# A four-layer graph network on one core: TensorE signals from a drain instead of from the last matmul

## The chip, the cores and the metric

The kernel runs on 1 core of one Trainium2 chip. The metric is the device time of one execution in microseconds; before the change the median of 3 runs is 5,466.43 us.

## What is computed

A graph of 6,250 nodes with 128 features and 200,000 edges goes through four pre-norm residual layers. `dst` is sorted, `src` is random.

```python
h = max(layernorm(x), 0); x = x + L0(h)   # h @ Wa.T + mean of h[src] over dst @ Wb.T + b
h = max(layernorm(x), 0); x = x + L1(h)   # sum over edges of w*(h[dst]-h[src]), w = sigmoid(relu((h[dst]-h[src])@W1+b1)@W2+b2); + indeg*(h@W4+b4)
h = max(layernorm(x), 0); x = x + L2(h)   # mean of relu(h@Wp.T+bp)[src] @ Wl.T + bl + h@Wr.T, elu, normalised, + h
h = max(layernorm(x), 0); x = x + L3(h)   # sum over edges of (h @ weight[etype])[src]*norm; + h@loop_weight
```

## The kernel before

The edges lie in 1,563 tiles of 128, one edge a partition, and tiles go in groups of four (`TPG`). There are two ways to sum over a destination.

The first is **gather and scatter**. POOL issues one indirect DMA per tile (line 1470) that fetches the 128 source rows from a table in HBM. VectorE builds a one-hot matrix of the destinations of each tile within a window of 128 nodes (lines 1863, 1869). TensorE multiplies the one-hot matrix with the gathered rows and accumulates in PSUM (`scatter`, lines 2530, 2533, 2537; `scatter_h`, 2511). The last matmul of a group increments `s_scat`. POOL waits for `s_scat` before it gathers into the group's slot again (5 slots in layers 0 and 2, 7 in layer 1, 10 in layer 3), VectorE before it writes a one-hot buffer again. When a window is full, it is copied, turned with the identity (`far_turn`, 2546 and 2548, `s_gturn`) and added to `acc`.

The second is **counting**. Where destinations are dense, VectorE writes pairs of one-hot matrices (1954, 1955, 1960, 1961), TensorE turns them into counts of edges between a block of sources and a few destinations (`count`, 2559, `s_count`), ScalarE takes the counts out (1632), and a pack matmul multiplies them with the node table (`pack_mm`, 2574, then 2584 and 2586). Layer 0 makes the early counts and multiplies at once. Layer 1 makes the late counts for layer 2 and stores them, layer 2 loads all of them.

Layer 1 has a longer chain for each group: SyncE fetches the destinations (`dst_flat`), VectorE makes a turned one-hot (1990), TensorE expands the destination rows (`expand`, 2597, `s_expand`), VectorE subtracts and weights (1998, 2003, "hidden"), ScalarE sums and takes the sigmoid (1681, 1686, "gates"), VectorE makes the gated one-hot (1863), TensorE scatters. Expansion stands one turn behind the gather, hidden and gates two, the scatter four.

Layer 3 has **dense steps** beside its gathers: `count3` (2469, 148 times), `mult3` (2481), `rels3` (2490), `put3` (2499), the latter three once for each of 13 bundles. VectorE's `pair3` (1908, 1909) waits for the count3 three tiles back. Between layers 2 and 3 lies a short stage of gathers for the heads (116 tiles), beside the relation products (2419).

All engines walk one list `plan`, written out by Python generators, and each engine's program takes its own kinds of step from it in that order. A planner's credit spreads the pack work evenly over the turns of groups. Every signal is a semaphore increment; on TensorE it is attached to the last matmul of a step:

```python
for t in range(m):
    last = pe.matmul(far3_banks[v % 3][:, 0:P], rows[:, slot, t, :], oneh[:, g % NONE_F, t, :],
                     start=start, stop=stop)
last.then_inc(s_scat.handle, 1)
```

Of the kernel before, what the change touches and what calls it, by code (L numbers as in the profile page):

```python
# [11 lines left out]
P = 128  # L12
TPG = 4
WIN = 64
# [51 lines left out]
def gnn_program(nc, ins, out):  # L66
# [15 lines left out]
    while len(bundles) < npk and (not bundles or bundles[-1][-1] < npk - 1):  # L82
        k0 = bundles[-1][-1] + 1 if bundles else 0
        n = max(m for m in range(1, npk - k0 + 1) if m * needed[k0 + m - 1] <= BUNDLE)
# [15 lines left out]
    while not heads or heads[-1][-1] < HEAD_END - 1:  # L100
        a = heads[-1][-1] + 1 if heads else ng3
        n = max([m for m in range(1, HEAD_END - a + 1) if n_nodes * (2 * a + m) * m * TPG * TPG <= HEAD_SPAN * nt * nt] + [1])
# [44 lines left out]
    with ExitStack() as ctx:  # L147
# [2202 lines left out]
        def tensor_program(pe):  # L2350
            pe.wait_ge(s_const.handle, n_const)
            for kind, st in plan:
# [110 lines left out]
                elif kind == "count3":  # L2463
# [4 lines left out]
                    for b, (q0, q1) in enumerate(((0, st["half"]), (st["half"], nb))):  # L2468
                        last = pe.matmul(ps[st["bank"] + b][:, 0:(q1 - q0) * w3], srow3[:, slot, :],  # L2469
                                         pairs3[:, slot, q0 * w3:q1 * w3], start=st["start"], stop=st["stop"])  # L2470
                    last.then_inc(s_count3.handle, 1)
                elif kind == "mult3":
                    q0, q1, width = st["q0"], st["q1"], st["width"]
                    if q0 == 0:
# [5 lines left out]
                    for q in range(q0, q1):  # L2480
                        last = pe.matmul(ps[4][:, 0:width], h[:, q, :], weights3[:, q, 0:width], start=q == 0, stop=q == nb - 1)  # L2481
                    if q1 == nb:
                        last.then_inc(s_mult3.handle, 1)
                elif kind == "rels3":
                    pe.wait_ge(s_sum3.handle, st["sum"])
                    if st["out_free"]:
# [2 lines left out]
                    for r in range(n_rel):  # L2489
                        last = pe.matmul(ps[4][0:st["slots"], P:2 * P], by_rel[:, :, r], wrel[:, r * P:(r + 1) * P],  # L2490
                                         start=r == 0, stop=r == n_rel - 1)
                    last.then_inc(s_rels3.handle, 1)
                elif kind == "put3":
                    n = st["slots"]
                    pe.wait_ge(s_place3.handle, st["place"])
                    pe.wait_ge(s_out3.handle, st["out"])
                    if st["add_free"]:
                        pe.wait_ge(s_add.handle, st["add_free"])
                    pe.matmul(ps[4][:, 2 * P:2 * P + WIN], out3[0:n, :], place[0:n, st["u"] % 2, 0:WIN], start=True, stop=True
                              ).then_inc(s_put3.handle, 1)  # L2500
                elif kind == "scatter_h":
                    g, m, slot = st["g"], tiles[st["g"]], st["slot"]
                    pe.wait_ge(s_one.handle, st["one"])
# [6 lines left out]
                    for t in range(m):  # L2510
                        last = pe.matmul(far3_banks[st["bank"]][:, 0:P], rows[:, slot, t, :], oneh[:, g % NONE_F, t, :],
                                         start=st["first"] and t == 0, stop=st["last"] and t == m - 1)
                    last.then_inc(s_scat.handle, 1)
                elif kind == "rels_h":
                    pe.wait_ge(s_hsum.handle, st["copy"])
                    by_rel = sums_head[:, st["half"], 0:st["n"] * P].rearrange("p (c r) -> p c r", r=n_rel)
                    for r in range(n_rel):
                        last = pe.matmul(far3_banks[st["bank"]][:, P:P + st["n"] * HEAD_WIN], wrel[:, r * P:(r + 1) * P], by_rel[:, :, r],
                                         start=r == 0, stop=r == n_rel - 1)
                    last.then_inc(s_hrel.handle, 1)  # L2520
                elif kind == "scatter":
                    g, v, m, slot = st["g"], st["v"], tiles[st["g"]], st["slot"]
                    pe.wait_ge(s_one.handle, st["one"])
                    pe.wait_ge(s_row[slot].handle, st["row"])
                    if st["first"] and st["add"]:
                        pe.wait_ge(s_add.handle, st["add"])
                    for t in range(m):
                        start, stop = st["first"] and t == 0, st["last"] and t == m - 1
                        if st["layer"] == 3:
                            last = pe.matmul(far3_banks[v % 3][:, 0:P], rows[:, slot, t, :], oneh[:, g % NONE_F, t, :],  # L2530
                                             start=start, stop=stop)
                        elif st["layer"] == 1:
                            last = pe.matmul(far_banks[v % 2][:, 0:P + 1], oneh[:, g % NONE_F, t, :],  # L2533
                                             rows_hp[slot][:, t, P:2 * P + 1], start=start, stop=stop)
                        else:
                            n_part = 3 * P + 1 if st["sums"] == 2 else 3 * P
                            last = pe.matmul(far_banks[v % 2][:, 0:n_part], onehb[:, g % NONE, t, :], rows_h3[slot][:, t, 0:n_part],  # L2537
                                             start=start, stop=stop)
                    last.then_inc(s_scat.handle, 1)
                elif kind == "far_turn":  # L2540
                    bank = far_banks[st["v"] % 2]
                    if st["layer"] == 1:
                        pe.wait_ge(s_glo.handle, st["lo"])
                    else:
                        pe.wait_ge(s_gev.handle, st["hi"])
                    last = pe.matmul(bank[:, 0:P], gsum[:, 0:P], ident[:, :], start=True, stop=True)
                    if st["sums"] == 2:
                        last = pe.matmul(bank[:, P:2 * P], gsum[:, P:P + 1].to_broadcast([P, P]), ident[:, :],
                                         start=True, stop=True)
                    last.then_inc(s_gturn.handle, 1)  # L2550
                elif kind == "count":
                    i, w, start, stop = st["i"], st["w"], st["start"], st["stop"]
                    pe.wait_ge(s_pair.handle, st["pair"])
                    for bank, q0, q1, evicted, signals, _ in st["parts"]:
                        if evicted:
                            pe.wait_ge(s_cev.handle, evicted)
                        rows_of_source = srow_late if st["late"] else srow
                        pair = pairs_late[:, i % 2, :] if st["late"] else pairs[:, i % NQS, :]
                        last = pe.matmul(ps[2 + bank][:, 0:(q1 - q0) * w], rows_of_source[:, i % NSR, :], pair[:, q0 * w:q1 * w],  # L2559
                                         start=start, stop=stop)  # L2560
                        if signals:
                            last.then_inc(s_count.handle, 1)
                elif kind == "pack_mm":
                    u, width, q0, q1 = st["u"], st["width"], st["q0"], st["q1"]
                    n_part = 3 * P + 1 if st["sums"] == 2 else 3 * P
                    if q0 == 0:
                        if st["layer"] == 0:
                            pe.wait_ge(s_cev.handle, st["cev"])
                        else:
                            pe.wait_ge(s_cld[u % 2].handle, st["cld"])  # L2570
                        if st["wev"]:
                            pe.wait_ge(s_wev.handle, st["wev"])
                    for q in range(q0, q1):
                        last = pe.matmul(ps[st["bank"]][0:width, 0:n_part], counts[:, u % 2, q, 0:width], h3[:, q, 0:n_part],  # L2574
                                         start=q == 0, stop=q == nb - 1)
                    if q1 == nb:
                        last.then_inc(s_pack.handle, 1)
                elif kind == "pack_turn":
                    u, width = st["u"], st["width"]
                    pe.wait_ge(s_place.handle, st["place"])  # L2580
                    pe.wait_ge(s_wev.handle, st["whi"])
                    if st["added"]:
                        pe.wait_ge(s_add.handle, st["added"])
                    last = pe.matmul(ps[1][:, 0:P], wsum[0:width, 0:P], place[0:width, u % 2, :], start=True, stop=True)
                    if st["sums"] == 2:
                        last = pe.matmul(ps[1][:, P:2 * P], wsum[0:width, P:P + 1].to_broadcast([width, P]),
                                         place[0:width, u % 2, :], start=True, stop=True)
                    last.then_inc(s_turn.handle, 1)
                elif kind == "expand":
                    g = st["g"]  # L2590
                    m, sl = tiles[g], g % 2
                    pe.wait_ge(s_oneT.handle, st["oneT"])
                    pe.wait_ge(s_pw[st["v"] % 2].handle, st["pw"])
                    if st["hid"]:
                        pe.wait_ge(s_hid.handle, st["hid"])
                    for t in range(m):
                        last = pe.matmul(ps_t[sl][:, t * P:(t + 1) * P], onehT[:, sl, t * P:(t + 1) * P], pwin[:, st["v"] % 2, :],  # L2597
                                         start=True, stop=True)
                    last.then_inc(s_expand.handle, 1)
                elif kind == "general":  # L2600
                    flag = outside_flag(pe, st["layer"])
                    with pe.If(flag):
                        general_tensor(pe, st["layer"], st["sums"])
                    if st["layer"] == 1:
                        pe.wait_ge(s_onecol.handle, 1)
# [29 lines left out]
```

## Time and profile before

| | |
|---|---|
| median of 3 runs | 5,466.43 us (5,464.44 to 5,467.47) |
| profiled execution, span | 6,426.8 us (its page gives no other time of it) |
| busy: PE, PEld, DVE, ACT, POOL | 60%, 46%, 46%, 22%, 62% of the span |
| mean granted TensorE clock | 0.761 |
| stages by POOL's gathers | layer 0: 107.8 to 1,217.8; layer 1: 1,304.2 to 3,643.1; layer 2: 3,696.3 to 4,293.8; heads: 4,340.8 to 4,510.9; layer 3: 4,526.4 to 6,404.8 us |

PE is TensorE's matmuls, PEld its weight loads, DVE VectorE, ACT ScalarE, POOL GpSimd, SP SyncE. The span of the profiled execution is 960 us longer than the median run. Busy time of PE is the union of matmuls whose ends are modelled. A tile's name in the rows is that of the memory under it (`third`, `rows`, `oneh`, `turned_words` are reused by several stages). "remote", or "another core or an unknown queue", is a wait whose releaser the trace does not tell. An f32 matmul of the program stands in the trace as two MATMUL rows with two LDWEIGHTS.

### The profile page before, as it was taken

The page shows a single profiled execution, that of the slowest core. Times are in us where ns is not written, and L with a number is a line of the kernel's source. Part 1 is how long each engine was busy: PE and PEld are TensorE (multiplying, and loading weights), DVE is VectorE, ACT ScalarE, POOL GpSimd, SP SyncE. Part 2 cuts the span into 40 slices and gives each one's busy share as a digit, 9 for nine tenths or more (in the row PEclk, how much of TensorE's full clock was granted, in tenths as well). Part 3 has the DMA queues.
Part 4 walks back from the last instruction along what each step waited for, and adds up shares of the span by engine and source line. Part 5 has one row for each costly group of instructions (what it writes and reads, how often), then busy time and mean ns, then how long its engine had stood idle before and what let it go on. Part 6 is the DMA issues. An engine that isn't in the chain of part 4 may idle for free.

```text
span 6426.8 us, 68888 instructions
## 1 busy us (share of the span) xinstructions
PE 3872.2 (60%) x20122; PEld 2959.4 (46%) x20154; DVE 2933.5 (46%) x9989; ACT 1413.8 (22%) x5474; POOL 3972.3 (62%) x4198
## 2 busy tenths in 40 slices
PE   4676766655555565555555578876565565665433
PEld 3333434445544454455455456653344444444332
DVE  7555544556555565556555633342333222222222
ACT  4222122333333333333333401121000000000000
POOL 4556666456666666666666466646566666666665
PEclk7778778777777777777777789998777777777666
DMA  3333333345455454544545455555211111111121
GB/s 107 96 101 110 111 105 116 107 140 155 143 150 148 147 150 144 154 145 141 159 144 151 123 184 198 195 181 178 69 46 46 45 47 45 46 45 46 46 61 46
DMA packets 323521, 734.49 MB, mean 114 GB/s; under 512 B 77056, under 2 KB 164124, under 8 KB 310860
## 3 DMA queue, kind: packets, MB, share of 16 engines
q0 software_dynamic: 172432, 405.32, 23.2%
q1 hardware_dynamic: 148700, 323.81, 14.9%
q8 instruction: 168, 2.75, 0.2%
q14 instruction: 205, 1.68, 0.1%
q10 hardware_dynamic: 2016, 0.92, 0.1%
HBM read 598.71 MB, written 131.05 MB: 114 GB/s over the span
## 4 chain that ended last, share of the span: by engine, by line
another core or an unknown queue 30%; PE 27%; DVE 19%; issue 15%; ACT 4%; DMA 2%; DVEq 1%; SPq 1%; ACTq 0%
PE ps L2574 8%; DVE oneh L1863 6%; PE ps L2559 3%; PE ps L2530 3%; PE ps L2537 2%; DVE ps L1998 2%; PE ps L2469 2%; PE ps L2597 2%; DMA third<-dst_flat 2%; ACT turned_words L1681 1%; DVE third L1990 1%; PE ps L2419 1%; DVE turned_words L1955 1%; DVE tmp L1954 1%
## 5 line engine op out<-in xcount | busy, mean ns | idle before, releaser
L1470 POOL DMA_INDIRECT rows<-tab_rel,third x1299 | 1247.0, 960 | 646.9 <-issue 367.1
L1470 POOL DMA_INDIRECT rows<-tab_h,idx_src x1086 | 1046.7, 964 | 723.4 <-issue 345.8
L1470 POOL DMA_INDIRECT rows<-tab_hp,idx_src x1120 | 1077.1, 962 | 622.5 <-issue 298.8
L2597 PE MATMUL ps<-third 128*128 128x128 f32 x3126 | 607.1, 353 | 501.6 <-issue 295.8
L2530 PE MATMUL ps<-oneh,rows 128*128 128x128 f32 x2598 | 489.1, 340 | 607.1 <-DVE oneh L1863 330.7
L2597 PEld LDWEIGHTS ps<-third 128*128 128x128 f32 x3126 | 539.6, 258 | 593.7 <-issue 355.3
L2574 PE MATMUL ps<-third,h 128*120 128x384 bf16 (+17 forms) x3773 | 715.0, 337 | 65.8 <-issue 34.6
L2530 PEld LDWEIGHTS ps<-oneh,rows 128*128 128x128 f32 x2598 | 432.6, 245 | 695.8 <-DVE oneh L1863 362.6
L1681 ACT ACTIVATE turned_words<-turned_words 128x128 f32<-128x128 f32 x1563 | 463.1, 300 | 690.8 <-DVE turned_words L2003 527.5
L2574 PEld LDWEIGHTS ps<-third,h 128*120 128x120 bf16 (+10 forms) x3773 | 487.8, 133 | 239.4 <-issue 61.3
L1470 POOL DMA_INDIRECT third<-tab_hp,idx_src x443 | 425.9, 961 | 231.7 <-issue 118.5
L1863 DVE TENSOR_SCALAR oneh<-iota_b,dst_rel,third 128x128 f32<-128x128 f32 x1299 | 356.5, 356 | 306.5 <-remote 244.6
L2533 PE MATMUL ps<-rows,oneh 128*128 128x129 f32 x2240 | 413.5, 333 | 90.6 <-issue 86.7
L1863 DVE TENSOR_SCALAR oneh<-iota_b,dst_rel,gate 128x128 f32<-128x128 f32 x1563 | 445.1, 359 | 17.0 <-ACT gate L1686 15.2
L2533 PEld LDWEIGHTS ps<-rows,oneh 128*128 128x128 f32 x2240 | 376.7, 248 | 102.1 <-issue 100.0
L2559 PE MATMUL ps<-turned_words,tmp 128*128 128x504 bf16 (+10 forms) x1108 | 330.0, 366 | 143.2 <-issue 69.5
L1632 ACT CAST h<-ps 128x245 bf16<-128x245 f32 (+13 forms) x554 | 233.1, 448 | 828.5 <-PE ps L2559 468.0
L1954 DVE TENSOR_SCALAR tmp<-tmp 128x128 bf16<-128x128 int16 x872 | 230.5, 265 | 312.4 <-PE ps L2559 168.4
L1998 DVE TENSOR_TENSOR ps<-ps,rows 128x512 f32<-128x512 f32 x280 | 193.7, 692 | 389.0 <-remote 318.3
L2481 PE MATMUL ps<-acc,h 128*128 128x128 f32 (+1 forms) x1274 | 219.3, 320 | 127.4 <-issue 94.6
L1681 ACT ACTIVATION_READ_ACCUMULATOR turned_words<-turned_words 128x1 f32 x1563 | 296.0, 189 | 0.0
L1955 DVE TENSOR_SCALAR turned_words<-tmp,key 128x245 bf16<-128x245 int16 (+10 forms) x872 | 289.9, 333 | 0.0
(279 smaller groups left out, 5495.4 us busy)
## 6 DMA issues: line engine op xcount, KB each, us to landing
third<-dst_flat SPq DMA_DIRECT2D x390, 256.0 KB
h<-cnt_d SPq DMA_DIRECT2D x48, 1568.0 KB
cnt_d<-h SPq DMA_DIRECT2D x29, 1568.0 KB
cnt_d<-third SPq DMA_DIRECT2D x19, 1568.0 KB
tab_rel<-third SPq DMA_DIRECT2D x49, 512.0 KB
rows<-tab_rel,third POOLq DMA_INDIRECT x1299
rows<-tab_hp,idx_src POOLq DMA_INDIRECT x1120
rows<-tab_h,idx_src POOLq DMA_INDIRECT x1086
```

Of the source, the lines that this page charges most:

```text
L1470: pool.indirect_dma_start(out=to[:, t, 0:n], out_offset=None, in_=table[:, :], in_offset=bass.IndirectOffsetOnAxis(ap=idx[:, col:col + 1], ...
L1632: act.copy(to[:, q0:q1, place:place + w], ps[2 + bank][:, 0:(q1 - q0) * w].rearrange("p (q w) -> p q w", w=w)).then_inc(s_cev.handle, 1)
L1681: last = act.activation(v, v, ACT.Copy, accum_out=zed[:, sl, t:t + 1])
L1863: last = dve.tensor_scalar(oneh[:, g % NONE_F, t, :], iota_b[:, :], dst_rel[:, col:col + 1], by, ALU.is_equal, ALU.mult)
L1954: dve.tensor_scalar(srow[:, i % NSR, :], iota_k[:, 0:P], src_row[:, i:i + 1], None, ALU.is_equal)
L1955: dve.tensor_scalar(pairs[:, i % NQS, 0:nb * w], iota_k[:, 0:nb * w], key[:, i:i + 1], None, ALU.is_equal).then_inc(s_pair.handle, 1)
L1998: dve.tensor_tensor(out=v, in0=v, in1=rows_hp[st["slot"]][:, 0:m, 0:P], op=ALU.subtract).then_inc(s_diff.handle, 1)
L2530: last = pe.matmul(far3_banks[v % 3][:, 0:P], rows[:, slot, t, :], oneh[:, g % NONE_F, t, :], start=start, stop=stop)
L2533: last = pe.matmul(far_banks[v % 2][:, 0:P + 1], oneh[:, g % NONE_F, t, :], rows_hp[slot][:, t, P:2 * P + 1], start=start, stop=stop)
L2559: last = pe.matmul(ps[2 + bank][:, 0:(q1 - q0) * w], rows_of_source[:, i % NSR, :], pair[:, q0 * w:q1 * w], start=start, stop=stop)
L2574: last = pe.matmul(ps[st["bank"]][0:width, 0:n_part], counts[:, u % 2, q, 0:width], h3[:, q, 0:n_part], start=q == 0, stop=q == nb - 1)
L2597: last = pe.matmul(ps_t[sl][:, t * P:(t + 1) * P], onehT[:, sl, t * P:(t + 1) * P], pwin[:, st["v"] % 2, :], start=True, stop=True)
```

## The change

Each place named below ends with a `drain` on TensorE that carries the increment, in place of the increment on the last matmul. A drain is an instruction of the queue that ends when the engine's earlier work is done, and what stands behind it in TensorE's queue starts after it. Early counts (layer 0), pack matmuls, their turn, and all node-wise steps keep their signals on the matmul. The order of instructions on every engine, and the number of matmuls, stay. In the built program there are 2,188 new drains: 988 behind `scatter`, 29 behind `scatter_h`, 391 behind `expand`, 444 behind late `count`, 145 behind `far_turn`, 148 behind `count3`, 13 each behind `mult3`, `rels3` and `put3`, 4 behind `rels_h`.

```diff
@@ count3, mult3, rels3, rels_h, scatter_h, scatter, far_turn, expand
-                    last.then_inc(s_count3.handle, 1)
+                    pe.drain().then_inc(s_count3.handle, 1)
...
-                        last.then_inc(s_mult3.handle, 1)
+                        pe.drain().then_inc(s_mult3.handle, 1)
...
-                    last.then_inc(s_rels3.handle, 1)
+                    pe.drain().then_inc(s_rels3.handle, 1)
...
-                    pe.matmul(ps[4][:, 2 * P:2 * P + WIN], out3[0:n, :], place[0:n, st["u"] % 2, 0:WIN], start=True, stop=True
-                              ).then_inc(s_put3.handle, 1)
+                    pe.matmul(ps[4][:, 2 * P:2 * P + WIN], out3[0:n, :], place[0:n, st["u"] % 2, 0:WIN], start=True, stop=True)
+                    pe.drain().then_inc(s_put3.handle, 1)
...
-                    last.then_inc(s_scat.handle, 1)
+                    pe.drain().then_inc(s_scat.handle, 1)
...
-                    last.then_inc(s_hrel.handle, 1)
+                    pe.drain().then_inc(s_hrel.handle, 1)
...
-                    last.then_inc(s_gturn.handle, 1)
+                    pe.drain().then_inc(s_gturn.handle, 1)
@@ count
-                        if signals:
+                        if signals and st["late"]:
+                            pe.drain().then_inc(s_count.handle, 1)
+                        elif signals:
                             last.then_inc(s_count.handle, 1)
@@ expand
-                    last.then_inc(s_expand.handle, 1)
+                    pe.drain().then_inc(s_expand.handle, 1)
```

## Rows read from the trace of the kernel before

**Rows 1.** The timeline of 4571 to 4600 us, POOL: start, length, instruction, idle before.
```profile
4576.14 0.94 POOL L1470 DMA_INDIRECT rows<-tab_rel,third  x1 [0.30 <-issue]
4577.39 0.94 POOL L1470 DMA_INDIRECT rows<-tab_rel,third  x1 [0.30 <-issue]
```

**Rows 2.** The line of the gathers, L1470: count, duration min/median/max in ns.
```profile
L1470 POOL DMA_INDIRECT rows<-tab_rel,third x1299: 938/944/1404, 4526.4 to 6403.8; - x186
L1470 POOL DMA_INDIRECT rows<-tab_hp,idx_src x1120: 940/946/1431, 1304.2 to 3638.4; - x187
L1470 POOL DMA_INDIRECT rows<-tab_h,idx_src x1086: 940/946/2048, 107.8 to 4292.9; - x181
L1470 POOL DMA_INDIRECT third<-tab_hp,idx_src x443: 940/946/1437, 1329.8 to 3642.2; - x148
```

**Rows 3.** The table of stages: busy us and count of each engine, granted clock.
```profile
core 0: us, PE busy (x) PEld busy (x) DVE busy (x) ACT busy (x) POOL busy (x), PEclk, DMA share, GB/s
0.00:107.80 107.80, 46.52 (x218) 38.66 (x219) 72.83 (x283) 53.74 (x117) 52.37 (x120) 0.81 0.47 137
107.80:1217.80 1110.00, 731.28 (x3481) 411.63 (x3481) 606.36 (x2681) 257.23 (x627) 667.90 (x691) 0.76 0.35 103
1217.80:1304.20 86.40, 63.32 (x386) 52.30 (x385) 53.56 (x260) 39.89 (x97) 11.82 (x15) 0.80 0.44 133
1304.20:3643.10 2338.90, 1339.03 (x7451) 1176.17 (x7481) 1340.63 (x3646) 800.24 (x3956) 1503.81 (x1564) 0.75 0.50 147
3643.10:3696.30 53.20, 20.11 (x123) 18.21 (x123) 39.03 (x104) 32.27 (x89) 0.02 (x1) 0.66 0.29 96
3696.30:4293.80 597.50, 498.86 (x2910) 367.31 (x2911) 220.83 (x1010) 66.72 (x203) 378.64 (x395) 0.93 0.57 193
4293.80:4340.80 47.00, 26.08 (x136) 17.90 (x134) 27.92 (x125) 25.52 (x73) 0.84 (x3) 0.75 0.44 141
4340.80:4510.90 170.10, 120.38 (x413) 63.32 (x412) 51.48 (x128) 33.41 (x64) 109.93 (x116) 0.83 0.53 180
4510.90:4526.40 15.50, 12.71 (x55) 8.69 (x54) 8.48 (x27) 2.87 (x6) 0.01 (x1) 0.89 0.45 175
4526.40:6404.80 1878.40, 1002.83 (x4895) 795.09 (x4893) 502.44 (x1691) 101.88 (x244) 1247.00 (x1299) 0.71 0.19 47
6404.80:6426.80 22.00, 11.05 (x67) 10.13 (x67) 9.98 (x37) 0.00 (x0) 0.00 (x0) 0.73 0.07 19
```

**Rows 4.** The same timeline, layer 3, PE and DVE around a late signal.
```profile
4574.55 1.48 PE L2469 MATMUL ps<-third 128*128 128x400 f32 x4
...
4591.12 0.28 DVE L1908 TENSOR_SCALAR third<-iota_b,turned_words 128x128 f32<-128x128 f32 x1 [17.62 <-remote]
```

**Rows 5.** The page: busy time by engine, and the chain's shares.
```profile
PE 3872.2 (60%) x20122; PEld 2959.4 (46%) x20154; DVE 2933.5 (46%) x9989; ACT 1413.8 (22%) x5474; POOL 3972.3 (62%) x4198
...
another core or an unknown queue 30%; PE 27%; DVE 19%; issue 15%; ACT 4%; DMA 2%; DVEq 1%; SPq 1%; ACTq 0%
```

**Rows 6.** POOL's waits, layer 1, then layer 3: us in total, times, longest.
```profile
POOL rows L1470 <- remote: 233.6, 115, 4.7
...
POOL third L1470 <- remote: 93.5, 48, 2.8
POOL rows L1470 <- PE ps L2533: 71.0, 26, 5.8
...
POOL rows L1470 <- remote: 228.8, 81, 5.9
POOL rows L1470 <- PE ps L2530: 27.0, 15, 4.2
```

**Rows 7.** The timeline in layer 1: ends of scatter groups and the next weight load.
```profile
2012.45 1.93 PE L2533 MATMUL ps<-rows,oneh 128*128 128x129 f32 x8
...
2013.96 0.36 PEld L2559 LDWEIGHTS ps<-tmp 128*128 128x128 bf16 x2
...
2016.52 1.12 PE L2533 MATMUL ps<-rows,oneh 128*128 128x129 f32 x8
...
2017.36 0.21 PEld L2559 LDWEIGHTS ps<-tmp 128*128 128x128 bf16 x2
```

**Rows 8.** The timeline in layer 2: end of a scatter group.
```profile
3906.72 0.81 PE L2537 MATMUL ps<-rows,oneh 128*128 128x384 bf16 x4
...
3907.21 1.02 PEld L2441 LDWEIGHTS ps<-wlT,acc 128*128 128x128 f32 x8
```

**Rows 9.** Lines L2524 and L147, PE's sequencer: duration ns min/median/max.
```profile
L2524 PEldq EVENT_SEMAPHORE  x784: 51/51/51, 142.0 to 6418.4; - x196
...
L147 PEldq DRAIN  x1: 687/687/687, 6421.4 to 6421.4; - x1
```

**Rows 10.** PE's groups by line in layer 2 (3696.3 to 4293.8 us).
```profile
L2574 PE MATMUL ps<-third,h 128*120 128x384 bf16 (+10 forms) x2270 | 418.6, 337 | 47.6 <-DMA h<-cnt_d 23.8 <-issue 23.2
...
L2546 PE MATMUL ps<-ident,gsum 128*128 128x128 f32 x56 | 11.3, 277 | 3.2 <-issue 3.2
```

More of the change, by code:

```diff
@@ L2538, in tensor_program @@
                                              start=start, stop=stop)
-                    last.then_inc(s_scat.handle, 1)
+                    pe.drain().then_inc(s_scat.handle, 1)
                 elif kind == "far_turn":
```

## The prediction

> **What bounds the kernel now.** I read the stage table first, then the gather line, POOL's waits, and a piece of the timeline where a signal is late. POOL issues one indirect gather per tile of 128 edges, and its rows show a fixed pace: a descriptor step of 0.94 us and 0.30 us of issue, so the starts stand 1.25 us apart [rows 1]. There are 4,064 gathers: 1,299 + 1,120 + 1,086 + 443 from tables [rows 2] and 116 in the heads stage [rows 3]. 4,064 x 1.25 = 5,080 us. The turnovers before, between and behind the five gather stages take 107.8 + 86.4 + 53.2 + 47.0 + 15.5 + 22.0 = 331.9 us [rows 3]. A kernel in which POOL never waits inside a stage would thus last 5,080 + 332 = 5,412 us.
>
> The profiled execution lasts 6,426.8 us, 1,015 us above that ledger, and the median run 5,466.4 us, only 54 us above it. The page gives no time of that execution beside its span. So nearly all that POOL waits in the profile is absent from the undisturbed runs, provided POOL's pace is the same there (a software loop with 0.94 us in every stage makes that likely; no row proves it). This is the reading on which everything below rests.
>
> What the extra 960 us are made of can be seen at one place. The last dense-step matmuls, count3, start at 4574.55 and end at 4576.03; then PE has nothing in flight, yet VectorE's L1908, which waits for a dense-step signal of PE, goes on only at 4591.12, after 17.62 us that the trace puts on a releaser it doesn't know [rows 4]. A signal of finished matmuls was at least 15 us late while PE stood idle. The same "unknown" makes 30% of the chain of waits [rows 5], and POOL's waits in layers 1 and 3 are mostly of that kind [rows 6]. The drain would look like the cure. But the ledger says that the undisturbed run can hold at most 54 us of such lateness inside the stages. I take it as mostly the profiler's own: PE has 40,276 of the 68,888 recorded instructions [rows 5]. The Trainium skill (NOTIFIC — the notification-queue block, section 7.1) has a rule of this kind: the block that writes the trace records holds its producers back inside rather than lose a record. It names no figure, and no row here shows the block itself.
>
> **The change, part by part.** It adds 2,188 drains to PE's queue, takes 2,188 increments off matmuls, and moves nothing. They are 1,017 behind scattered groups (a group is up to four tiles: 173, 391, 99, 29 and 325 in the stages' order), 391 behind expansions, 444 behind late counts, 145 behind far turns, 187 behind dense steps, 4 behind the heads' relation sums.
>
> *Price of one drain.* No row shows a drain inside a stream of PE, so I bound it. What it forbids is visible. In layer 1 at the slow clock a group of 8 matmuls starts at 2012.45 and takes 1.93, to 2014.38, while the next weight load has begun at 2013.96: 0.42 us of overlap [rows 7]. At the fast clock: 2016.52 + 1.12 = 2017.64 against 2017.36, 0.28 us. In layer 2, bf16: 3906.72 + 0.81 = 3907.53 against 3907.21, 0.32 us [rows 8]. The drain takes that overlap away. Its own step costs at least a sequencer's, 0.05 us [rows 9]; the drain at the program's end took 0.69 us, waiting included. Lower bound 0 (where PE would wait next anyway), upper bound 0.69 + 0.42 = 1.1 us; I take overlap plus 0.05: 0.33 us warm f32, 0.37 us in layer 2, 0.47 us cold. The Trainium skill (TensorE: Matmul & The Clock Gate, section "Part 2: What happens when you issue a matmul") puts the part of one matmul's latency that a following one hides at about 0.175 us; by that figure, an estimate, the layer 2 term below would be 127 x 0.175 = 22 us instead of 47.
>
> *Layer 2 (3696.3 to 4293.8).* POOL's 395 gathers need 395 x 1.25 = 494 us; PE is busy 498.9 us there, at a clock of 0.93 [rows 3]: PE is as full as POOL. It carries 2,270 of the pack matmuls for 418.6 us beside the scatters [rows 10]. 99 groups and 28 turns (56 matmuls of L2546 [rows 10], two a turn) add 127 drains x 0.37 = 47 us. There is no cover for them. PE's 499 + 47 = 546 us becomes the bound. I take three quarters, +35 us, since some drains fall where PE waits for a load (23.8 us before pack matmuls [rows 10]) or for VectorE.
>
> *Layer 0 (107.8 to 1217.8).* POOL needs 691 x 1.25 = 864 us, PE is busy 731.3 [rows 3]. 173 scatters and 44 turns: 217 x 0.37 = 80 us, to 811. Early counts keep their matmul signals. Cover 133 us; cost 0, with up to 20 us where several engines take turns.
>
> *Layer 1 (1304.2 to 3643.1).* 391 scatters, 391 expansions, 444 late counts and 65 turns: 1,291 drains, at 0.33 to 0.47 us 426 to 607 us of PE. PE is busy 1,339 of the profile's 2,339 us, and POOL needs 1,563 x 1.25 = 1,954 [rows 3]. PE would hold 1,765 to 1,946 us of that. The cover is 1,954 - 1,339 = 615 us, used to between 70% and nearly all. The group's chain runs expansion, VectorE's hidden step, ScalarE's gates, one-hot, scatter; its slots give POOL seven groups less the four that the scatter lies behind. Behind a drain wait the next expansion and its VectorE step. Cost 0 in the likeliest case, up to +80 if the slow clock holds.
>
> *Heads and layer 3.* Heads: 29 groups x 0.47 = 14 us on 120 of PE against POOL's 145 [rows 3]; hidden. Layer 3: 325 + 187 = 512 x 0.47 = 241 us on 1,002.8, together 1,244 against POOL's 1,299 x 1.25 = 1,624; hidden.
>
> *Late signals removed.* Worth between 0 and the 54 us above; I take 0 in the sum.
>
> Sum: +35 us on the median, 5,466.4 + 35 = **5,501 us**. In the profiled execution the same +35 applies only if the lateness stays; if drains escape the disturbance, its span falls by much more than any run gains, and that must not be read as the kernel's gain.
>
> **The rivals.**
>
> *Faster, the other side.* The lateness of PE's signals is real in undisturbed runs too. It decides if more than 35 us of the 54 in the stages, and of the 332 in the turnovers, is such waiting. Removing all 54 and a tenth of the turnovers (33) against 35 of drains gives 5,466 - 87 + 35 = 5,414 us; half of it 5,458. I put the case at 5,430. For: the 15 us at a place where PE was idle can't be its work. Against: the ledger. An extreme form needs POOL's pace to be quicker without the profiler, so that POOL waits there as much of the time as here: 1,015 / 6,427 = 16% of 5,466, of which half would be 430 us, giving 5,036. Nothing but the 0.30 us of issue speaks for it.
>
> *No change.* Layer 2's PE has more room than its busy time says, since ends of matmuls are modelled and tails overlap waits: 5,466 within 11 us.
>
> *PE bounds layer 1 too.* 1,946 us of 1,954, at the clock of 0.75, leaves nothing for waits in order: +35 + 80 = 5,581 us. Against: a fuller PE was granted a faster clock (0.93 in layer 2, PE busy 83%; 0.75 in layer 1, 57%) [rows 3].
>
> *The clock falls in layer 2.* Were its clock to go from 0.93 to layer 1's 0.75, 499 us would become 619, and +120 + 47 gives 5,633. The Trainium skill (TensorE: Matmul & The Clock Gate, section "Part 1: The HAM clock gate (the "warmup" mystery)") says that the half clock is the default and activity lifts it; by that rule more standing still costs clock. The traced 83% of PE and standings of 0.4 us make it unlikely here.
>
> **How the numbers follow.** A measurement of this kernel can tell 0.2%, 11 us, from no change. Chances: slower through layer 2 (5,485 to 5,530) 0.36; layer 1 too 0.09; clock 0.03; no change 0.21; faster at 5,405 to 5,455 0.28; extreme 0.03. Faster 0.31, same 0.21, slower 0.48. The range reaches from the faster case's 5,405 to 5,570, which holds most of the layer 1 case; it leaves out the extreme, the clock case and the tails. Cases of both signs hold the chance, so the likeliest one's own range is 5,485 to 5,530.
>
> **What would show it.** Of the profile after: POOL's starts still 1.25 us apart, else the ledger falls. In the layer 2 window PE busy under 499 + 47 and its window no shorter than 520 us by itself would fit; a run time below 5,455 makes the profiler theory wrong. In layer 1 the weight load behind each scatter starts after the group's last matmul ends, by 0.05 to 0.3 us: that is the drain's price, and above 0.5 it is mis-sized. Waits on unknown releasers that vanish while the run time stays show that they belonged to the profile. Waits on unknown releasers that vanish together with run time show the rival.

## The result and the profile after

The changed kernel takes 5,510.5 us (median of 4 runs, 5,505.8 to 5,512.0) against 5,467.0 us: a ratio of 1.0075 with a 95% interval of 1.0062 to 1.0087, 43.5 us slower. The forecast was 5,501.

The profile after has a span of 5,509.1 us, next to its run time of 5,510.9, while the span of the profile before had been 960 us above the runs. That makes the two profiles poor partners: most of what differs between them isn't the change. The stage table of the profile after answers to [rows 3] (stages cut at POOL's first and last gather; columns as there).

```profile
105.80:1036.30 930.50, 736.18 (x3526) 389.94 (x3525) 604.46 (x2699) 256.70 (x632) 675.05 (x691) 0.87 0.40 125
...
1109.10:3099.40 1990.30, 1412.53 (x7509) 1110.33 (x7540) 1353.58 (x3667) 808.65 (x3979) 1514.56 (x1564) 0.80 0.58 173
...
3146.30:3662.90 516.60, 483.40 (x2895) 351.28 (x2895) 219.22 (x1010) 66.99 (x203) 379.40 (x395) 0.98 0.64 222
3662.90:3713.90 51.00, 29.10 (x150) 19.52 (x150) 27.91 (x125) 25.52 (x73) 0.82 (x2) 0.77 0.44 138
3713.90:3858.90 145.00, 130.44 (x497) 76.09 (x496) 62.96 (x165) 37.88 (x72) 109.91 (x116) 0.95 0.65 230
3858.90:5498.20 1639.30, 1063.35 (x4920) 806.24 (x4919) 513.13 (x1714) 102.50 (x242) 1243.44 (x1299) 0.76 0.19 54
```

The chain of the page after is led by POOL's gathers, one behind the other, and has no unknown releaser, against 30% of it in [rows 5].

```profile
POOL 49%; issue 19%; PE 15%; DVE 7%; DMA 3%; PEld 3%; PEldq 2%; ACT 1%; DVEq 1%; SPq 1%; POOLq 0%; ACTq 0%
```

What POOL waits for on the new drains (`PEq L2539`, the drain behind a scatter), in layer 0, layer 1, layer 2 and layer 3:

```profile
POOL rows L1470 <- PEq L2539: 54.3, 30, 11.5
...
POOL rows L1470 <- PEq L2539: 5.8, 19, 0.3
POOL third L1470 <- PEq L2539: 3.3, 11, 0.3
...
POOL rows L1470 <- PEq L2539: 31.1, 47, 1.9
...
POOL rows L1470 <- PEq L2539: 0.3, 1, 0.3
```

Two stages have such waits, layers 0 and 2. Part of each is only the usual 0.3 us between gathers. The waits alone don't tell which were there before, since the profile before can't be used for it.

### The profile page after: what moved, and what is told of

The parts are those of the page before. It is cut to its first block, busy times and chain, and to the rows that moved or that the text cites. A ratio compares the mean times of both kernels' runs of the same rounds, so it can differ in the third digit from the quotient of the medians.

```text
span 5509.1 us, 71076 instructions
## 1 busy us (share of the span) xinstructions
PE 3970.5 (72%) x20122; PEld 2851.0 (52%) x20154; DVE 2937.2 (53%) x9989; ACT 1419.0 (26%) x5474; POOL 3987.5 (72%) x4198
## 4 chain that ended last, share of the span: by engine, by line
POOL 49%; issue 19%; PE 15%; DVE 7%; DMA 3%; PEld 3%; PEldq 2%; ACT 1%; DVEq 1%; SPq 1%; POOLq 0%; ACTq 0%
POOL rows L1470 42%; PE ps L2576 9%; POOL third L1470 6%; PE ps L2537 2%; PE ps L2419 1%; PE ps L2559 1%; DVE turned_words L1955 1%; DVE tmp L1954 1%; PEld ps L2599 1%; DMA rows<-tab_hp,idx_src 1%; PEldq L2539 1%; PEld ps L2533 1%; DMA third<-dst_flat 1%; DMA third<-tab_hp,idx_src 1%; PEld ps L2576 1%
## 5 line engine op out<-in xcount | busy, mean ns | idle before, releaser
L1470 POOL DMA_INDIRECT rows<-tab_rel,third x1299 | 1243.5, 957 | 395.9 <-issue 395.6
L1470 POOL DMA_INDIRECT rows<-tab_h,idx_src x1086 | 1054.6, 971 | 447.3 <-issue 354.1
L1470 POOL DMA_INDIRECT rows<-tab_hp,idx_src x1120 | 1085.5, 969 | 358.8 <-issue 335.1
L2599 PE MATMUL ps<-third 128*128 128x128 f32 x3126 | 564.0, 337 | 363.5 <-DVE third L1990 311.0
L2530 PEld LDWEIGHTS ps<-oneh,rows 128*128 128x128 f32 x2598 | 419.8, 246 | 628.5 <-issue 452.0
L2576 PE MATMUL ps<-third,h 128*120 128x384 bf16 (+17 forms) x3773 | 701.8, 337 | 36.6 <-DMA h<-cnt_d 22.7
L2599 PEld LDWEIGHTS ps<-third 128*128 128x128 f32 x3126 | 483.6, 237 | 467.0 <-DVE third L1990 363.8
L1470 POOL DMA_INDIRECT third<-tab_hp,idx_src x443 | 428.2, 967 | 134.8 <-issue 131.5
L2533 PE MATMUL ps<-rows,oneh 128*128 128x129 f32 x2240 | 402.3, 335 | 67.2 <-issue 62.3
L2533 PEld LDWEIGHTS ps<-rows,oneh 128*128 128x128 f32 x2240 | 349.0, 238 | 122.7 <-issue 113.4
L2559 PE MATMUL ps<-turned_words,tmp 128*128 128x504 bf16 (+10 forms) x1108 | 304.3, 340 | 85.5 <-DVE turned_words L1955 46.8
L2469 PE MATMUL ps<-third 128*128 128x400 f32 (+1 forms) x592 | 273.7, 592 | 27.2 <-issue 22.9
```

Source lines behind the costliest of these rows:

```text
L1470: pool.indirect_dma_start(out=to[:, t, 0:n], out_offset=None, in_=table[:, :], in_offset=bass.IndirectOffsetOnAxis(ap=idx[:, col:col + 1], ...
```

## The experiments

### One stage at a time

Each run takes the changed kernel and keeps its drains in some stages only; elsewhere the signal is back on the matmul.

```diff
-                    pe.drain().then_inc(s_scat.handle, 1)
+                    (pe.drain() if ("scatter", st["layer"]) in DRAINED else last).then_inc(s_scat.handle, 1)
```

and in the same way for the far turns, expansions, late counts, heads and dense steps. (The line with the set puts the lines of these kernels one below those of the changed one: the scatter's drain is L2540.)

*Layer 0 only.*

> Drains only in layer 0 (behind its 173 scattered groups and 44 far turns), everything else signals from the matmul. Theory of the prediction (layer 2 pays, layer 0 has 133 us of cover): +0 to +10 us on the 5,467 us of the kernel before. Theory B, read from the profile after, where POOL waits 54 us on the drains of layer 0's scatters but 31 us in layer 2: layer 0 pays most, +20 to +35 us. In the profile, both expect late signals and the long waits on unknown releasers to be gone in layer 0 alone and to stay from layer 1 on.

*Layer 1 only.*

> Drains only in layer 1 (391 scattered groups, 391 expansions, 65 turns, 444 late counts: 1,291 of the 2,188). Theory of the prediction and theory B: hidden, within 8 us of the kernel before. A theory that every drain costs a little wherever it stands (43.5 us over 2,188, 20 ns each) gives +26 us. In the profile, the unknown waits should be gone in layer 1 alone if the drain cures them where it stands.

*Layer 2 only.*

> Drains only in layer 2 (99 scattered groups and about 30 far turns). Theory of the prediction: this is the whole loss, +25 to +45 us. Theory B: +8 to +20 us. Every drain alike: +3 us.

*Heads and layer 3 only.*

> Drains only in the heads stage and layer 3 (29 + 4 and 325 + 187). Theory of the prediction and theory B: hidden behind POOL's gathers, within 6 us of the kernel before. Every drain alike: +11 us.

Measured against 5,472.3 us of the kernel before on the same chip:

| drains in | drains | us | ratio, 95% interval |
|---|---|---|---|
| layer 0 | 220 | 5,484.4 | 1.0026 (1.0015 to 1.0038) |
| layer 1 | 1,294 | 5,471.7 | 1.0000 (0.9991 to 1.0009) |
| layer 2 | 129 | 5,500.5 | 1.0057 (1.0043 to 1.0070) |
| heads and layer 3 | 545 | 5,467.5 | 0.9993 (0.9984 to 1.0003) |

(The counts are those of each stage's own steps; the windows by POOL's gathers had cut off a few.) Layer 2 costs 28 us, layer 0 12 us, and 1,839 of the 2,188 drains cost nothing. 28 + 12 = 40, close to the 43.5 of the whole. A price per drain wherever it stands is refuted: layer 1 has ten times the drains of layer 2. Layer 2 is the main place, as the prediction had it, and theory B fails in both: its 8 to 20 us for layer 2 were too low, its 20 to 35 us for layer 0 too high. Layer 0 pays a little more than the +0 to +10 that the prediction's theory gave it.

The runs of layers 0 and 1 missed one expectation, that late signals would stay in the stages without drains. The profiles of all four show none anywhere, and each span is within 6 us of the median of its runs. The lateness was not cured by the drains; it wasn't there.

### Whose the late signals were

> The kernel before, unchanged, profiled once more. Four profiles of kernels that keep most or nearly all matmul signals had spans within 5 us of their run times and no unknown waits, also in the stages without a drain. Theory 1, the late signals of the first profile belonged to that one profiled execution: span near 5,470 us, unknown waits near 0%. Theory 2, they belong to the kernel before whenever it is profiled, and any drain in the stream cures them: span again near 6,400 us.

The unchanged kernel ran in 5,467.5 us, with a span of 5,465.6 us (15 runs of it have a median of 5,467.5). Theory 2 falls. Its chain has no unknown releaser:

```profile
POOL 59%; issue 20%; PE 11%; DVE 5%; DMA 3%; ACT 1%; SPq 1%; DVEq 0%; POOLq 0%; ACTq 0%
```

Its stages, which are the partners that the profile after needed:

```profile
106.50:1021.50 915.00, 705.58 (x3526) 402.37 (x3526) 605.80 (x2698) 256.67 (x632) 674.40 (x691) 0.87 0.42 127
...
1094.60:3086.80 1992.20, 1236.77 (x7541) 1100.43 (x7539) 1348.62 (x3668) 803.42 (x3979) 1516.41 (x1564) 0.81 0.59 173
...
3132.40:3631.00 498.60, 474.99 (x2969) 365.46 (x2970) 224.91 (x1037) 67.58 (x206) 378.55 (x395) 0.98 0.68 234
3631.00:3667.70 36.70, 14.99 (x77) 10.19 (x76) 22.32 (x98) 24.80 (x70) 0.83 (x3) 0.70 0.51 152
3667.70:3812.70 145.00, 129.36 (x508) 78.82 (x506) 63.77 (x167) 37.88 (x72) 109.93 (x116) 0.92 0.66 230
3812.70:5454.80 1642.10, 997.77 (x4907) 800.21 (x4907) 511.06 (x1712) 102.48 (x242) 1246.24 (x1299) 0.76 0.21 54
```

Beside the table after: layer 2 goes from 498.6 to 516.6 us, the turnover behind it from 36.7 to 51.0, layer 0 from 915.0 to 930.5. Layer 1, the heads and layer 3 keep their lengths within 3 us. 18.0 + 14.3 + 15.5 = 47.8 us, against 43.5 of the run times.

Layer 2 in this profile is 499 us long with PE busy for 475.0 (95%) and POOL needing 494: nearly as full as the prediction had read it from the disturbed profile. The chain of this stage together with the turnover behind it, first of the kernel before, then of the run with drains in layer 2 alone, shows the bound pass from two engines to one (the pack matmuls are L2574 and L2577; the last line is cut off by the view):

```profile
by line: PE ps L2574 42.9%; POOL rows L1470 23.8%; issue 8.8%; PE ps L2537 7.8%; DMA rows<-tab_h,idx_src 4.0%; PE ps L2584 1.4%; PE ps L2441 1.4%; DMA h<-cnt_d 1.3%; PE ps L2546 0.8%; DVE h L1756 0.7%; DVE tmp L2217 0.7%; ACT h L1556 0.5%; 
```

```profile
by line: PE ps L2577 59.3%; PE ps L2538 10.1%; issue 8.7%; PEld ps L2577 5.4%; PE ps L2587 2.1%; PE ps L2442 2.0%; DMA h<-cnt_d 1.3%; PE ps L2547 1.0%; PEld ps L2538 0.8%; PEldq L2551 0.7%; DVE h L1757 0.7%; DVE tmp L2218 0.7%; DVE tmp L220
```

POOL held 23.8% of the chain before; with drains it is not among the lines that this view names. POOL now waits for PE: within the stage, before and with drains in layer 2,

```profile
POOL rows L1470 <- PE ps L2537: 2.1, 7, 0.3
```

```profile
POOL rows L1471 <- PEq L2540: 32.2, 49, 1.9
```

### Which drains of layer 2, and what of a drain

> Drains only behind the 99 scattered groups of layer 2. If the loss of 28 us in layer 2 is PE's lost time, it goes by the count of drains: 28 x 99/128 = +22 us. If it is the far turns' chain, near 0.

> Drains only behind the far turns of layer 2 (some 29). By the count of drains +6 us; if the turns' chain carries the loss, +20 us or more.

Against 5,467.5 us, scatter drains alone give 5,493.0 (1.0043, 1.0029 to 1.0057), +25.5 us; turn drains alone 5,471.9 (1.0006, 0.9997 to 1.0015), +4.4. That fits the counts, 99 to 30, as far as the intervals tell (+16 to +31 us and -2 to +8 us), and leaves no special cost of the turns' chain.

> Layer 2 as in the run with drains there alone, but the signal stays on the last matmul and the drain behind it carries none. Theory of the prediction (the standstill of PE costs): +25 to +31 us, as with the signal on the drain. Rival (the signal that leaves later, by a sequencer's step, costs): near 0.

```diff
-                    pe.drain().then_inc(s_scat.handle, 1)
+                    last.then_inc(s_scat.handle, 1)
+                    if ("scatter", st["layer"]) in DRAINED:
+                        pe.drain()
```

5,500.5 us (1.0060, 1.0046 to 1.0073), +33 us. The run with the signal on the drain had the same 5,500.5; its +28 differs only because the kernel before then took 5,472.3 us instead of 5,467.5. Where the signal leaves from costs nothing that these runs can tell; the standstill of TensorE behind a drain makes the price.

### Three runs that met another chip

In one set of runs the chip was another one, and on it the kernel before, without any profile, has a median of 6,359.2 us. Ratios below are to that.

> Two drains instead of one behind each scattered group and far turn of layer 2. The second finds the engine empty, so it shows a drain's own step without the lost overlap. In the profile after, the next weight load starts 0.07 or 0.20 us after the last matmul's end. If 0.07 is the step, 128 more steps give +28 + 9 = +37 us; if 0.20, +28 + 25 = +53 us; if a second drain is free, +28 us.

```diff
+                    if ("scatter", st["layer"]) in DRAINED:
+                        pe.drain()
                     (pe.drain() if ("scatter", st["layer"]) in DRAINED else last).then_inc(s_scat.handle, 1)
```

(and so for the turns.) 6,397.1 us, 1.0056 (1.0036 to 1.0077), +38 us. The same edit with one drain wasn't run on this chip, so what the second adds isn't measured as a time of the kernel. Its trace shows it: from the first matmul of a scatter group of four to the first pack matmul behind it, where nothing was late, it took 0.96 to 0.98 us, against 0.89 or 0.90 in the run with one drain on the other chip. A second drain thus costs about 0.07 us; its own record lasts 13 ns at the median.

> Leaves out 3 of every 7 pack matmuls of layer 2 (28 of 49 blocks of sources are kept), no drains: its sums over the counted edges of layer 2 are partial. It takes 48 x 21 x 0.163 us = 164 us of PE from layer 2. If PE is as full as POOL there, the stage can't get much shorter than POOL's 494 us, so mostly the turnover behind it shrinks: -5 to -30 us against the kernel before.

> The same with drains in layer 2. Theory of the prediction (drains cost because PE has no room in layer 2): with 164 us of room they are hidden, within 5 us of the run without drains. Rival (a drain delays the signal, POOL's slots or the chain by itself): still some +28 us above it.

```diff
-                    for q in range(q0, q1):
+                    for q in (range(q0, q1) if st["layer"] == 0 else range(q0, q1, 2)):
```

Plain 6,345.2 us (0.9978, 0.9963 to 0.9993), with drains 6,368.2 (1.0014, 0.9999 to 1.0030): the drains still cost 23 us, where my theory said within 5. As it stands this speaks against the theory that room on PE hides them. But on this chip a drain is another thing. A scatter group of the half-drained kernel, and what follows on PE and POOL:

```profile
3928.43 0.81 PE L2538 MATMUL ps<-rows,oneh 128*128 128x384 bf16 x4
3935.00 2.19 PEld L2577 LDWEIGHTS ps<-third,h 128*120 128x120 bf16 x8 [6.14 <-issue]
3935.01 2.49 PE L2577 MATMUL ps<-third,h 128*120 128x384 bf16 x7 [5.76 <-issue]
3935.22 0.94 POOL L1471 DMA_INDIRECT rows<-tab_h,idx_src  x1 [2.28 <-PEq L2540]
```

The matmuls end at 3929.24 and PE goes on 5.76 us later. The drain waits as long as the late completion takes and stops PE meanwhile. In this trace 35 of the 99 drains behind scatters end over 1 us after the matmuls' modelled end, up to 15.4 us after it. The delays come to 127 us, and to 38 us more behind the 30 turns: as much as the 164 us that the edit was to free. In the run with drains in layer 2 alone on the other chip each of these drains ends 0.02 us after the matmuls. The longest drain behind a scatter shows it too, first of this kernel, then of the one with drains in layer 2 on the other chip (duration min/median/max in ns; a drain's time runs from where PE's sequencer reaches it, so its median says little):

```profile
L2540 PEldq DRAIN  x99: 748/3088/19070, 3663.8 to 4259.6; - x99
```

```profile
L2540 PEldq DRAIN  x99: 722/3088/4138, 3147.2 to 3671.5; - x99
```

In layer 2, POOL waited for these signals in all 87.6 us without drains (two rows) and 109.0 us with them, 21 us more, close to the 23:

```profile
POOL rows L1471 <- remote: 72.9, 32, 4.0
POOL rows L1471 <- PE ps L2538: 14.7, 6, 8.3
```

```profile
POOL rows L1471 <- PEq L2540: 109.0, 52, 10.0
```

So the pair doesn't decide about room on an undisturbed chip; that experiment stays open there. It does show that in layer 2 a drain is no cure for a late completion.

### The free drains alone

> The drains of the change where they were free (layer 1, heads, layer 3: 1,841 of the 2,188, by the runs 0 and 0 us), matmul signals in layers 0 and 2. Which of two chips it meets isn't known beforehand. On the chip where the kernel before takes 5,467 to 5,472 us: theory of the prediction, within 8 us of it, and 40 us under the full change. On the chip where it takes 6,359 us: if a drain's signal is on time where a matmul's is late (in layer 2 the drained scatters of that chip had theirs), POOL's over-long gaps of layers 1, heads and 3 vanish (341 + 23 + 229 us there), so some 5,770 us; if the lateness lies elsewhere, near 6,350 us.

It met a chip on which the kernel before takes 5,473.0 us, and ran in 5,474.0 (1.0004, 0.9995 to 1.0013): free, as expected, and 0.66% under the full change's 5,510.5. (By the built counts it holds 1,839 drains, not 1,841.) It doesn't beat the kernel before, and no drained version did. What the drains of layers 1 and 3 do on the chip of the late completions wasn't seen.

## Why the prediction was right, and where it was not

**The place and the sum held.** "There is no cover for them. PE's 499 + 47 = 546 us becomes the bound. I take three quarters, +35 us". Layer 2 alone measured +28 us, by scatters and turns about as their counts, and the chain changed from POOL and PE to PE. The stage grew by 18 us, to 516.6, a little under the 520 that the prediction named as a sign, and the turnover behind it by 14: the sum had not said that a part of the cost would show only where PE's last pack work ends after POOL's last gather. The reading of [rows 3] that carried this, PE busy 498.9 us against 494 of POOL, was right by some luck: it came from a disturbed execution, and the clean one shows 475.0 against 494. The total of 43.5 us lies near 35 in part because layer 0 added 12 that the sum had put at 0.

**The price of a drain** was taken as the lost overlap plus 0.05 us. The profile of the changed kernel has it in the open. In layer 1, an expansion, the scatter behind it and a late count (PE, then PEld, from two views of the same stretch):

```profile
1501.14 1.16 PE L2599 MATMUL ps<-third 128*128 128x128 f32 x8 [1.20 <-DVE third L1990]
1502.53 1.13 PE L2533 MATMUL ps<-rows,oneh 128*128 128x129 f32 x8 [0.23 <-issue]
1503.89 0.46 PE L2559 MATMUL ps<-tmp 128*128 128x504 bf16 x2 [0.23 <-issue]
```

```profile
1502.50 0.97 PEld L2533 LDWEIGHTS ps<-rows,oneh 128*128 128x128 f32 x8 [0.39 <-issue]
1503.86 0.13 PEld L2559 LDWEIGHTS ps<-tmp 128*128 128x128 bf16 x2 [0.39 <-issue]
```

The first group ends at 1501.14 + 1.16 = 1502.30, the next weight load starts at 1502.50: 0.20 us behind the end, with 0.28 us of overlap lost [rows 7], 0.48 us where 0.33 was taken. In layer 2:

```profile
3303.59 0.81 PE L2537 MATMUL ps<-rows,oneh 128*128 128x384 bf16 x4
...
3304.47 1.00 PEld L2576 LDWEIGHTS ps<-third,h 128*120 128x120 bf16 x7 [0.46 <-issue]
```

3304.40 to 3304.47, 0.07 us behind the end, so 0.32 + 0.07 = 0.39 where 0.37 was taken.

The measured 28 us over 129 drains are only 0.22 us each, and the traces show why. What delays PE is the distance from one matmul group's start to the next one's, and the start of a weight load is a poor measure of it: the load also ran ahead of its own matmul. Layer 2 of the unchanged kernel in the clean profile, then of the run with drains in layer 2 alone:

```profile
3304.28 0.81 PE L2537 MATMUL ps<-rows,oneh 128*128 128x384 bf16 x4
3304.93 3.58 PE L2574 MATMUL ps<-third,h 128*120 128x384 bf16 x21
...
3313.76 0.39 PE L2546 MATMUL ps<-ident,gsum 128*128 128x128 f32 x2
3313.98 0.81 PE L2537 MATMUL ps<-rows,oneh 128*128 128x384 bf16 x4
```

```profile
3303.82 0.81 PE L2538 MATMUL ps<-rows,oneh 128*128 128x384 bf16 x4
3304.71 1.34 PE L2577 MATMUL ps<-third,h 128*120 128x384 bf16 x7
...
3308.39 0.38 PE L2547 MATMUL ps<-ident,gsum 128*128 128x128 f32 x2
3309.01 0.81 PE L2538 MATMUL ps<-rows,oneh 128*128 128x384 bf16 x4 [0.23 <-issue]
...
3314.49 0.81 PE L2538 MATMUL ps<-rows,oneh 128*128 128x384 bf16 x4
3315.53 1.13 PE L2442 MATMUL ps<-wlT,acc 128*128 128x128 f32 x8 [0.23 <-issue]
```

Before, a scatter group's start is followed by the next matmul's after 0.65 us; with the drain it takes 0.89 (0.24 lost) in 62 of the 96 groups of four in that trace, and 1.03 or more (mostly 1.04, 0.40 lost) in the others. Behind a turn, 0.22 becomes 0.62 (0.40 lost). 62 x 0.24 + 34 x 0.40 + 30 x 0.40 = 40 us, an estimate from these rows. In the clean profile of the unchanged kernel PE also waited 7.7 us in layer 2 for gathered rows; with drains it has no such wait, since POOL is then ahead:

```profile
PE ps L2574 <- DMA h<-cnt_d: 22.9, 1, 22.9
PE ps L2584 <- DVE place L1967: 8.0, 1, 8.0
PE ps L2537 <- DMA rows<-tab_h,idx_src: 7.7, 8, 2.3
```

40 - 7.7 = 32 us, against the 32 us by which stage and turnover grew. This account is read from the two traces; no run of its own tests it. So the term that was mis-sized is the price, 47 us for about 40. The quarter taken off was near the mark, but not for the reason given: the load wait of 23.8 us is one wait that stands mostly before the first gather, and no scatter falls into it (22.9 us in the clean profile, until 3138.74, with the first scatter group at 3145.98). The figure of the Trainium skill (TensorE: Matmul & The Clock Gate, section "Part 2: What happens when you issue a matmul"), 0.175 us a drain and an estimate of 22 us in all, comes out below the measured 28 to 33 us. The trace has 0.16 us for the overlap of one matmul group's modelled end with the next group's start (0.81 - 0.65), near that figure; a drain costs another 0.08 or 0.23 us behind the end.

**Layer 1 hidden** held, at the fast clock's price of 0.48 us too: 1,294 x 0.48 = 621 us is within the clean profile's cover, 1,954 - 1,237 = 717 us. PE busy rose from 1,236.8 to 1,412.5 us of a stage that kept its length (1,992.2 and 1,990.3), at a clock of 0.81 before and 0.80 after. Its stage length is POOL's, 1,563 x 1.25 = 1,954 us and some waits. **Heads and layer 3 hidden** held. **Layer 0** was given "cost 0, with up to 20 us where several engines take turns"; it measured 12. What was short is the cover: 133 us in total isn't 133 us where needed. POOL's waits for scatters in layer 0 grew from 35.8 us to 56.3 with drains there alone. That they come from the five slots and from pack work ahead of the scatters on PE is argued, not shown.

```profile
POOL rows L1470 <- PE ps L2537: 35.8, 18, 11.4
```

```profile
POOL rows L1471 <- PEq L2540: 56.3, 31, 12.7
```

**The step that failed** is the one that explained the extra 960 us of the profile before: "I take it as mostly the profiler's own". It is not. A profile costs this kernel nothing that shows (span 5,465.6 beside a run of 5,467.5), and on another chip the undisturbed time itself is 6,359 us. The extra 960 us belong to a chip or its condition. That the profile before was taken on such a chip is inferred, not shown: its mean granted clock of 0.761 and its 30% of unknown releasers are like those of that chip's profiles (0.750 to 0.762, 23 to 29%), where the undisturbed ones have 0.81 to 0.82 and none. The prediction's sign for it, unknown waits that vanish while the run time stays, came true and still could not tell the profiler from the chip. The rule of the Trainium skill that I leaned on (NOTIFIC — the notification-queue block, section 7.1) is not shown at work by any run here. The conclusion drawn from the step, that the runs at 5,466 us hold little such lateness, was right because it came from the ledger and not from the cause. The ledger was itself rough: 5,080 us of gathers hold (starts still 1.25 us apart), but the clean turnovers are 106.5 + 73.1 + 45.6 + 36.7 + 10.8 = 273 us, not 332, and POOL waits some 113 us inside the stages, not 54.

**The rivals.** Faster: fell with the clean profile of the kernel before, whose chain has no unknown releaser; there was no late signal to cure. PE bounding layer 1: fell, stage length unchanged. The clock: layer 2's stayed at 0.98 with and without drains.

## What to carry to other kernels

A drain on TensorE is paid in overlap: what matters isn't how many there are but whether the stage has TensorE time to spare, so make the ledger by stage. 129 drains in a stage where TensorE was 95% busy cost 28 us, 1,839 in stages bound by gathers cost none. Spare time on average isn't always enough: 220 drains in layer 0, where TensorE was 77% busy, cost 12 us. To price such a standstill, measure from one matmul's start to the next one's start, not from where a weight load begins. And hold the span of a profile against the undisturbed time before reading its waits; where they are far apart, take the profile again before you explain the waits or mend the kernel for them.

## What the runs showed of the hardware that was not expected

On one chip the same program takes 6,359 us instead of 5,467 to 5,473, with POOL's pace unchanged (its gathers' descriptor step 947 to 949 ns at the median there, 944 to 946 here) and TensorE's completions late. In the rows of the profile before, which was probably taken on that chip, work that waited for finished matmuls went on at least 15 us after them while PE was idle [rows 4]; in the half-drained kernel on that chip PE went on 5.76 us after the matmuls before a drain had ended. What holds the completions back is open. Signals on matmuls and signals on drains were both late. On the undisturbed chips the shown weight loads behind a drain start 0.07 or 0.20 us after the last matmul's modelled end, and the next matmul 0.08 or 0.23; both occur in layer 1 and in layer 2, and what chooses between them wasn't tried. In the changed kernel the drain's own record ends 0.02 us after that end behind all 988 scatters, but in layer 2 it begins some 3 us before it at the median, so its length isn't its cost.
